# Feature products of a projective-memory layer: weights folded into the decay factor, chunks added on GpSimd, one product per token tile, and new planner constants for layer 1

## The reference, cut to what matters

```python
scores = einsum('bihd,bjhd->bhij', q, k) * scale         # 16 heads of 16, causal softmax, times v
write_lines = exterior(w1, w2); read_lines = exterior(r1, r2)   # 6 numbers per token and head, unit length
Jw = einsum('bthi,ij->bthj', write_lines, J)
inc_sq = einsum('bihp,bjhp->bhij', read_lines, Jw) ** 2
weights = where(j < i, decays[h] ** (i - j), 0)
mem_score = sum(inc_sq * weights, axis=-1)
gated = mean_h(sigmoid(mem_score * mem_scale) * sigmoid(x @ memg_w + memg_b))
out = (seq_out + gated * (x @ memv_w + memv_b)) @ out_w + out_b
```

## Time and profile before

| | |
|---|---|
| median of 3 runs | 4106.52 us |
| profiled execution, its own time | 4099.16 us |
| its span, first to last instruction | 4096.4 us |
| TensorE matmul busy | 94% of the span |
| VectorE, ScalarE, GpSimd busy | 77%, 65%, 54% |
| mean granted TensorE clock | 0.969 |

### The profile page before, as it was taken

One profiled execution on the slowest core, in us unless ns is written; L12 is line 12 of the kernel. 1 busy time (PEld: TensorE's weight loads), 2 busy tenths in 40 slices (PEclk: granted clock), 3 DMA queues, 4 the chain that ended last, 5 costly groups with the idle time before them and its releaser, 6 DMA issues.

```text
span 4096.4 us, 62172 instructions
## 1 busy us (share of the span) xinstructions
PE 3843.2 (94%) x19744; PEld 2326.3 (57%) x19744; DVE 3171.2 (77%) x6071; ACT 2653.7 (65%) x4142; POOL 2205.0 (54%) x1724
## 2 busy tenths in 40 slices
PE   7999999999999999997989999999999999999998
PEld 3656665656565655655545565555555555555554
DVE  3789999999999999999485766857667576685763
ACT  6777778777878878775246465565655546555454
POOL 4787998988999999998131312313132131321311
PEclk9999999999999999998989999999999999999999
DMA  4444554444555555555221122211222212221111
GB/s 156 134 138 162 164 164 154 151 153 160 165 163 169 159 168 159 156 163 183 83 71 56 48 72 56 87 56 59 67 58 79 56 57 66 61 80 56 56 46 27
DMA packets 251030, 442.10 MB, mean 108 GB/s; under 512 B 25860, under 2 KB 80596, under 8 KB 249812
## 3 DMA queue, kind: packets, MB, share of 16 engines
q1 hardware_dynamic: 250708, 438.14, 34.9%
HBM read 366.39 MB, written 69.21 MB: 106 GB/s over the span
## 4 chain that ended last, share of the span: by engine, by line
PE 54%; DVE 10%; ACT 6%; issue 6%; DMA 0%; POOL 0%; DVEq 0%; SPq 0%; ACTq 0%; POOLq 0%
PE ps L1403 7%; PE ps L1506 6%; PE ps L1514 6%; PE ps L1365 5%; PE ps L1384 5%; PE ps L1434 3%; PE ps L1267 3%; PE ps L1316 3%; DVE ps L1901 2%; PE ps L1440 2%; PE ps L1277 2%; DVE ps L1923 2%; PE ps L1487 1%; PE ps L1445 1%; ACT L1531 1%
## 5 line engine op out<-in xcount | busy, mean ns | idle before, releaser
L2146 POOL TENSOR_TENSOR drive<-du,b_wide 128x1024 f32<-128x1024 f32 x512 | 1201.8, 2362 | 200.1 <-DVE held L1901 116.0
L2181 POOL TENSOR_SCALAR_AFFINE_SELECT exps<-exps 128x256 f32<-128x256 f32 x512 | 217.6, 426 | 1373.0 <-ACT exps L1531 1372.2
L1531 ACT ACTIVATE exps<-ps 128x1024 f32<-128x1024 f32 (+3 forms) x768 | 620.9, 810 | 487.2 <-PE ps L1384 460.4
L1531 ACT ACTIVATE ps<-delta,neg_a 128x512 f32<-128x512 f32 x1024 | 682.0, 685 | 151.3 <-DVE heavy L1879 137.1
L1923 DVE CUSTOM_DVE_ANT_0 ps<-ps,later 128x128 f32<-128x128 f32 (+3 forms) x1024 | 483.6, 512 | 194.8 <-PE ps L1365 190.2
L1316 PE MATMUL ps<-p_all,heavy 128*128 128x128 f32 x3072 | 440.9, 280 | 71.4 <-DVE heavy L1879 64.0
L1316 PEld LDWEIGHTS ps<-p_all,heavy 128*128 128x128 f32 x3072 | 363.3, 144 | 241.5 <-DVE heavy L1879 117.7
L1879 DVE TENSOR_TENSOR heavy<-c_wide,ps 128x512 f32<-128x512 f32 x704 | 468.6, 671 | 8.1 <-issue 4.0
L1901 DVE TENSOR_TENSOR_SCAN ps<-ps,carry,drive 128x512 f32<-128x512 f32 x352 | 441.7, 1273 | 32.4 <-ACT ps L1531 32.1
L1901 DVE TENSOR_TENSOR_SCAN ps<-ps,drive 128x512 f32<-128x512 f32 x352 | 420.6, 1215 | 48.7 <-ACT ps L1531 46.9
L1926 DVE TENSOR_REDUCE smax<-ps 128x2 f32<-128x1024 f32 x256 | 312.4, 1220 | 116.4 <-PE ps L1365 113.8
(11 more groups left out here) (193 smaller groups left out, 6562.9 us busy)
## 6 DMA issues: line engine op xcount, KB each, us to landing
b_wide<-bc_dram SPq DMA_DIRECT2D x512, 256.0 KB, 3.4
c_wide<-bc_dram SPq DMA_DIRECT2D x512, 256.0 KB, 3.5
stacks<-parts SPq DMA_DIRECT2D x192, 256.0 KB, 2.4
qs<-stacks SPq DMA_DIRECT2D x128, 192.0 KB
ks<-stacks SPq DMA_DIRECT2D x128, 192.0 KB, 4.3
x_row<-in_x SPq DMA_DIRECT2D x14, 1024.0 KB, 7.9
resid<-mix SPq DMA_DIRECT2D x9, 1024.0 KB, 5.4
x_row<-resid SPq DMA_DIRECT2D x9, 1024.0 KB, 5.8
```

The costliest lines, as they stand in the source:

```text
L1531: return nc.scalar.activation(out_, in_, func, **kw)
L2146: G.tensor_tensor(drive[:, g % DRIVE_SLOTS, :, :], du[:, e, :, :], wide(b_wide[:, g % B_SLOTS, :], MD), ALU.mult).then_inc(driven, 1)
```

## The change

Once, at the head, VectorE derives from `sumpq` one factor per partition and chunk (weight times decay, kept in the columns of the parameter `ew`, which are no longer needed), and sets the weights in the first chunk of `sumpq` to 1. The product `prod` then takes that factor in place of the decay, so it carries the weight already. GpSimd adds chunk 1 and then chunk 2 onto chunk 0 (a new task `sum`, two for each batch and half), and `ms` makes one product per token tile in place of three. TensorE waits for the factors before its planned list. The planner's length of `ms` becomes 0.5 from 1.1, it is told that VectorE empties `pa` and `pb` after ScalarE, and `LEAD`, `LAG` and all of `SPANS` are new.

```diff
-LENGTH = {..., "ms": 1.1,
+LENGTH = {..., "ms": 0.5,
...
-LEAD = 20
-LAG = 3
-SPANS = {"early": (-46, -22), "late": (-24, 8), "second": (-4, 20), "mlp": (14, 86), "close": (8, 28)}
+LEAD = 24
+LAG = 5
+SPANS = {"early": (-40, -30), "late": (-20, 0), "second": (4, 24), "mlp": (20, 86), "close": (20, 24)}
...
-            add("v", unit, EMPTY_V[kind], place[unit], (("a" if kind == "qk" else "p"),) + unit, *v)
+            add("v", unit, EMPTY_V[kind], place[unit], (("a" if kind in ("qk", "pa", "pb") else "p"),) + unit, *v)
...
+            for ch in range(1, FCH):
+                add("g", ("sum", b, c, ch), 1.27, place["fr", b, c, ch] + 1, ("v", "fr", b, c, ch))
             for i in range(2):
-                dense(("ms", b, c, i), ("v", "fr", b, c, FCH - 1))
+                dense(("ms", b, c, i), ("g", "sum", b, c, FCH - 1))
... TensorE
             pe.wait_ge(params_more_in, 16)
+            pe.wait_ge(setup_v, 2)
...
-                    drained(pe, plan, ("fr", b, c, FCH - 1), "v")
-                    pick = param("sumpq").rearrange("p (c h) -> p c h", c=FCH)
+                    pe.wait_ge(prod_summed, (FCH - 1) * (NC * b + c + 1))
                     for j in range(2):
                         tt = 2 * i + j
-                        for ch in range(FCH):
-                            last = mm(bank[:, j * H:(j + 1) * H], prod[:, ch, tt * P:(tt + 1) * P],
-                                      pick[0:FR, ch, :], start=(ch == 0), stop=(ch == FCH - 1))
+                        last = mm(bank[:, j * H:(j + 1) * H], prod[:, 0, tt * P:(tt + 1) * P], param("sumpq")[0:FR, 0:H],
+                                  start=True, stop=True)
... VectorE, at the head
             dve.wait_ge(params_more_in, 16)
+            times = param("ew")[0:FR, 0:FCH]
+            dve.wait_ge(setup_v, 1)
+            link("v", V.tensor_reduce(times, param("sumpq")[0:FR, :].rearrange("p (c h) -> p c h", c=FCH), AX_X, ALU.max))
+            link("v", V.tensor_scalar(times, times, param("decay")[0:FR, :], None, ALU.mult))
+            V.tensor_scalar(param("sumpq")[0:FR, 0:H], param("sumpq")[0:FR, 0:H], 1.0, None, ALU.min).then_inc(setup_v, 1)
... VectorE, unit fr
-                    V.scalar_tensor_tensor(prod[:, ch, :], gsum[:, ch, 0:HALF], rate, bank[0:FR, :], ALU.mult, ALU.mult)\
+                    V.scalar_tensor_tensor(prod[:, ch, :], gsum[:, ch, 0:HALF], rates[:, ch:ch + 1], bank[0:FR, :], ALU.mult,
+                                           ALU.mult)\
                         .then_inc(drained_v, 1)
... GpSimd
+                elif kind == "sum":
+                    c, ch = task[2:]
+                    drained(pool, plan, ("fr", n, c, ch), "v")
+                    if ch > 1:
+                        pool.wait_ge(prod_summed, (FCH - 1) * (NC * n + c) + ch - 1)
+                    G.tensor_tensor(prod[:, 0, :], prod[:, 0, :], prod[:, ch, :], ALU.add).then_inc(prod_summed, 1)
```

More of the change, by code:

```diff
@@ L424 @@
 SCORES = {P: 0.26, 2 * P: 0.32, 3 * P: 0.37, HALF: 0.43}
-LENGTH = {"xt": 0.55, "qk": 1.8, "pa": 1.6, "pb": 1.35, "lt": 0.5, "jw": 0.6, "fw": 0.5, "fr": 0.5, "ms": 1.1,
+LENGTH = {"xt": 0.55, "qk": 1.8, "pa": 1.6, "pb": 1.35, "lt": 0.5, "jw": 0.6, "fw": 0.5, "fr": 0.5, "ms": 0.5,
           "zt": 0.55, "wo": 1.8, "e1": 0.47, "e2": 0.47, "f1": 1.85, "o": 3.55}
@@ L940, in build @@
         gsum_set = sem("gsum_set")
+        prod_summed = sem("prod_summed")
         q_in = [sem(f"q_in{i}") for i in range(SLOTS)]
@@ L1904, in _ @@
             plan = L1_PLAN
-            scale, rate = param("scale"), param("decay")[0:FR, :]
+            scale, rate, rates = param("scale"), param("decay")[0:FR, :], param("ew")[0:FR, 0:FCH]
             by_head = "p (h d) -> p h d"
```

## The result

The changed kernel takes 4034.6 us, the median of 4 runs (4030.6 to 4049.6); the kernel before, run beside it, takes 4105.1 us. The ratio is 0.9834, with a 95% interval from 0.9818 to 0.9851: 68 us or 1.7% faster. The profiled execution has a span of 4031.5 us against 4096.4.

What follows compares the result with a forecast made beforehand. TensorE was taken to bound layer 1. The terms -31 - 8 + 1 + 2 + 8 - 4 = -32 us took the profiled 4099 us to 4067, and 7.4 us for the median of runs gave 4074; range 4040 to 4106.

Steps and rivals of the forecast that it cites:

- Part 1: In layer 1, 256 of the 384 ms matmuls and their loads leave TensorE: -31 us.
- Part 2: In layer 1, shorter ms pairs cause less TensorE time at 1.2 GHz behind them: -8 us, bounds 0 and -17.
- Part 3: In layer 1, 32 additions on GpSimd make ms come at least 1.3 us later, mostly covered: +1 us.
- Part 4: At the head, three small VectorE instructions delay the first scan and TensorE's list, mostly covered by idle time: +2 us.
- Part 5: With LEAD 24, TensorE waits at the first sm of some pairs for q and k to land: +8 us.
- Part 6: In the late stretch, new SPANS, LAG and order of pa and pb stay nearest to no change: -4 us.
- The first: The new lists also close TensorE's gaps in layer 1's late stretch: 4062 to 4027 us, typically 4045; chance 0.26.
- The forecast's own sign of being wrong: Layer 1's idle time plus lost clock on TensorE, 188 us, moves by more than 30 us in either direction.
- The second rival: TensorE's freed time turns into waits, as the late stretch hangs on the memory term's longer chain: 4104 us; chance 0.12.
- the third, the slots: TensorE waits for a DMA before the first sm of 61 pairs, 1 us each: 4128 us; chance 0.12.

Runs made afterwards that it cites:

- the folded kernel: The changed kernel with LEAD, LAG, SPANS and the order of pa and pb as before; 4103.0 us, ratio 0.9967 to the kernel before.

## Why the forecast was wrong

The forecast was -32 us; the ratio gives -68.

- **Part 1** (-31) was right: 31 us of work, and 33 us by the run with three products. It is worth that in the new lists; in the old ones most of it became idle time.
- **Part 2** (-8) has the mechanism, and about its size: by the same lists with three products the cause is worth 13. That the sum of layer 1 gives 8 as well (0.41 x (161.5 - 142.1)) is of one execution each and partly luck. The half that was taken had no row behind it, and one reading was off: the ten stretches behind pairs of before are 55 us and not 41, since the one from 2115 us on lasts 17 us.
- **Part 3** (+1): nothing, by the run without the additions.
- **Part 4** (+2): the first scan is 1.1 us later, and layer 0 ends 5 us earlier. In the 15 kernels with the new head the first scan starts 0.3 us earlier to 1.1 us later than before. Over the 18 kernels layer 0 ends between 1947 and 1960 us, and the three with the old head have 1952.0, 1955.5 and 1959.3, so this is scatter that no run here explains.
- **Part 5** (+8): 0.7 us. The mechanism is real and costs 20.8 us of waits in other lists; in this one it does not come up.
- **Part 6** (-4) is the step that failed. "Nearest to no change, as both have reasons" weighed the constants, and the order of `pa` and `pb` was given no price of its own. It is a correction: the list of before put VectorE in front of a bank that its own program may not touch until ScalarE has been there. The row that points at it is the wait of z for `pt`, 40.9 us in VectorE's waits from 2160 to 3900 us (64.5 with vals); no term of the forecast goes back to it, though these waits were there to read in the trace of before. It would not have given the price, since the rule took 38.5 us of these waits away and 21 us of time. By the experiments the order is worth 21 us before, 41 behind the folding and 27 in the change. On the folded kernel with the new order `LEAD`, `LAG` and `SPANS` together bring another 14 us by the ratios (0.9868 to 0.9834), whose intervals overlap. Taken together, the new lists (parts 5 and 6, +4 in the forecast) are worth 34 us on the kernel before and 55 on the folded one (0.9967 to 0.9834).

**The rivals.** The first, that the new lists also close the gaps of the late stretch, had the time (4062 to 4027) and part of the place: of the 21 us of idle time that go, 9 are the gap of 1.3 us at `lt`, which is gone in seven batches with the order alone and in the change. What spoke against it in the forecast, a chain "that no constant shortens", was mistaken in this: a part of the chain was VectorE standing at z for ScalarE, and the order of one list took it out. So no constant had to shorten it. The forecast's own sign of being wrong, idle plus lost clock of layer 1 moved by more than 30 us, came by a hair: its lost clock is half of the time at 1.2 GHz, so 21 us of idle time and 10 of clock make 31; with 0.41 in place of the half it is 29. (Its 86 us for that term come from a clock rounded to 0.96; half of 161.5 is 81, and at the 41% that part 2 uses it is 66.) The second rival, freed time that turns into waits, is what the folding alone shows, and the third, the slots, what `LEAD` 24 shows with the old `SPANS`; each needed lists that the change does not have.

## What to carry to other kernels

Where a change tells a planner of a wait that the engine's program makes anyway, read that engine's own waits, and what stands behind them in its queue, before giving the new order a price; TensorE's row names only the last link. The sum of these waits is no price by itself: 38 us less of them were 21 us of time here. A gain in instructions is kept only if the lists let it: here 28 us of work less became 31 us more idle time in the old lists. Constants of a planner are judged together: `LAG` alone and `SPANS` alone gained nothing where both gained 0.4%, and `LEAD` and `LAG` without `SPANS` cost 1.6%.

## What was not expected of the hardware

With the same instructions in layer 1 the time at 1.2 GHz was anything from 101 us (`LAG` and `SPANS` new, `LEAD` 20) to 243 us (the old `SPANS` but for `second`), by the order of the work alone. At 41% lost that is 58 us, where idle time moved by 15 us between the same two kernels (104 and 119 us). The other executions agree: the mean clock was 0.975 to 0.978 in the first kernel and 0.959 to 0.965 in the second. In the two lists with the least idle time (77.5 and 78.5 us, three products each) it is over 170 us. So the granted clock is a column of its own in such a comparison, and it wants more than one execution of each kernel.
